# Attention scores over stacked high and low parts, and weighing in 32 bits

## The reference

```
x = x + 0.5 * ffn(layernorm(x))
x = x + attention(layernorm(x))
x = x + 0.5 * ffn(layernorm(x))
```

```
q, k, v = inputs @ w_q.T, inputs @ w_k.T, inputs @ w_v.T     # 16 heads of 16
scores = einsum('bqhd,bkhd->bhqk', q, k)                     # causal, -inf above the diagonal
attn = softmax(scores / sqrt(256))
ctx = einsum('bhqk,bkhd->bqhd', attn, v)
return ctx @ w_o.T + b_o
```

## Time and profile before

| | |
|---|---|
| median of 3 runs | 439.52 us (436.39 to 440.93) |
| the profiled execution | 440.74 us |
| its span, first to last instruction | 438.6 us |
| TensorE busy | 408.5 us (93%) |
| DVE, ACT, GpSimd busy | 300.8, 257.1, 247.7 us |
| mean granted TensorE clock | 0.973 of full speed |
| attention stage | from about 161 to 292 us |

### The profile page before, as it was taken

The page is one execution under the profiler, slowest core; times in us unless marked ns, Lnnn a source line. Parts: engine busy times, 40 slices in busy tenths (PEclk is TensorE's granted clock), DMA queues, the critical chain, the costliest instruction groups (busy, mean ns, idle before and its releaser), DMA issues.

```text
span 438.6 us, 10176 instructions
## 1 busy us (share of the span) xinstructions
PE 408.5 (93%) x2911; PEld 333.9 (76%) x2912; DVE 300.8 (69%) x613; ACT 257.1 (59%) x638; POOL 247.7 (56%) x307
## 2 busy tenths in 40 slices
PE   7768999999999889799999999888799999999996
PEld 4536888888888867588887888764488888888884
DVE  6767996865556697777677676966365575556566
ACT  2706885555655455788787787822155655655552
POOL 5136445866467349657777577210365586754850
PEclk9679999999999999989999999996999999999999
DMA  8929931111211630000000000007551212112136
GB/s 278 371 68 347 389 100 59 47 51 60 59 48 36 190 109 1 1 1 2 4 1 0 0 0 0 1 1 252 153 184 49 62 37 72 60 48 52 44 103 208
DMA packets 25738, 38.90 MB, mean 89 GB/s; under 512 B 3056, under 2 KB 20720, under 8 KB 25712
## 3 DMA queue, kind: packets, MB, share of 16 engines
q1 hardware_dynamic: 19088, 24.41, 16.3%
q0 software_dynamic: 4544, 12.07, 9.4%
q10 hardware_dynamic: 2080, 2.10, 1.4%
HBM read 29.37 MB, written 9.19 MB: 88 GB/s over the span
## 4 chain that ended last, share of the span: by engine, by line
PE 65%; DVE 12%; DMA 10%; issue 5%; ACT 3%; POOL 2%; SPq 1%; DVEq 0%; ACTq 0%; POOLq 0%
PE bank L1301 24%; PE bank L1323 12%; PE bank L1459 7%; PE bank L1470 4%; PE bank L1311 3%; DMA xn_scratch<-arena 3%; PE bank L1224 3%; DMA w_out<-y_scratch 3%; PE bank L1426 2%; PE bank L1277 2%; PE bank L1506 2%; DMA arena<-xn_scratch,gather_row 2%; DVE w_lo L876 1%; DMA y_scratch<-arena,scatter_row 1%; PE bank L1460 1%
## 5 line engine op out<-in xcount | busy, mean ns | idle before, releaser
L509 POOL DMA_INDIRECT arena<-xn_scratch,gather_row x46 | 50.8, 1105 | 72.7 <-PE bank L1277 42.1
L515 POOL DMA_INDIRECT y_scratch<-arena,scatter_row x42 | 60.2, 1434 | 34.3 <-ACT arena L681 31.2
L1301 PE MATMUL bank<-w_hi,xT_hi 128*128 x184 | 62.6, 421 | 1.2 <-ACT xT_hi L640 1.2
L990 DVE TENSOR_TENSOR wo_lo<-w_out,wo_hi 128x1024 fp32r<-128x1024 f32 x46 | 60.8, 1321 | 4.1 <-PE bank L1323 1.9
L995 DVE TENSOR_TENSOR gT_lo<-bank,gT_hi 128x512 fp32r<-128x512 f32 x46 | 31.7, 689 | 39.3 <-ACT gT_hi L655 39.2
L1301 PE MATMUL bank<-w_hi,xT_lo 128*128 x184 | 58.1, 397 | 0.0
L1301 PE MATMUL bank<-w_lo,xT_hi 128*128 x184 | 57.8, 395 | 0.0
L593 POOL TENSOR_TENSOR k_head<-k_hi,head_mask 128x256 fp32r<-128x256 f32 x64 | 38.7, 625 | 29.1 <-PE bank L1460 22.2
L648 ACT ACTIVATE arena<-bank 128x512 f32<-128x512 f32 x46 | 27.5, 598 | 45.7 <-PE bank L1301 45.7
L670 ACT ACTIVATE wo_hi<-w_out 128x1024 fp32r x46 | 48.8, 1060 | 6.0 <-issue 4.1
L979 DVE TENSOR_TENSOR xT_lo<-bank,xT_hi 128x256 fp32r<-128x256 f32 x46 | 19.5, 424 | 39.0 <-ACT xT_hi L640 38.9
(11 more groups left out here) (180 smaller groups left out, 968.8 us busy)
## 6 DMA issues: line engine op xcount, KB each, us to landing
w_raw<-in_win_t SPq DMA_DIRECT2D x8, 1024.0 KB, 9.7
w_out<-in_wout_t SPq DMA_DIRECT2D x16, 512.0 KB, 8.0
w_out<-y_scratch SPq DMA_DIRECT2D x16, 256.0 KB, 4.9
xn_scratch<-arena ACTq DMA_DIRECT2D x2, 1024.0 KB, 8.7
x<-in_x SPq DMA_DIRECT2D x4, 256.0 KB, 3.6
out<-x SPq DMA_DIRECT2D x4, 256.0 KB, 2.1
arena<-xn_scratch,gather_row POOLq DMA_INDIRECT x46, 3.5
y_scratch<-arena,scatter_row POOLq DMA_INDIRECT x46, 3.0
```

The source lines that it names most:

```text
L509: pool.indirect_dma_start(out=xb[j % 2][:, :], out_offset=None, in_=xn_dram, in_offset=bass.IndirectOffsetOnAxis(ap=gather_row[:, j:j + 1] ...
L515: pool.indirect_dma_start(out=y_dram, in_=y[j % 2][:, :], in_offset=None, out_offset=bass.IndirectOffsetOnAxis(ap=scatter_row[:, j:j + 1], ...
L990: dve.tensor_tensor(wo_lo[:, :, :], w_out[:, bass.ds(e, 1), :, :].rearrange("p o c d -> p (o c) d"), wo_hi[u][:, :, :].bitcast(F32), ALU.s ...
L1301: last = pe.matmul(bank[2 * half + u][:, :], tok[u][:, k, :], wts[:, bass.ds(e, 1), k, half * H:(half + 1) * H], start=(part == 0 and k == ...
```

## The change

- **Scores.** The heads of a chunk are laid out anew (`lay_heads` permutes the weights' columns) so that a group of 64 rows holds 4 heads as (number within the head, head). SP then copies, from SBUF to SBUF, each half of the chunk into `q_stack` and `k_stack`: 16 rows of `q_hi`, 16 of `q_hi` again, 16 of `q_lo`, against `k_hi`, `k_lo`, `k_hi`. A head's score is now one product over 48 rows (0 to 47 or 64 to 111) that sums all three parts. Each copy is 64 rows of 1 KB; there are 12 for each chunk. `mask_keys` and `k_head` are gone. Head scores also use 256 columns for each head (`HEAD_KEYS`), into banks 2 and 6 in turn.
- **Weighing.** `v` and the turned probabilities stay 32-bit; each head and block has one product of 16 columns. The turned probabilities are only copied, one head on DVE and one on ACT. Context sums lie in bank 5 alone, and `divide` is one DVE multiplication from that bank.
- **Order.** The loop over batches is written out as 32 + 3 steps. A chunk is projected five pairs ahead. Values of tiles 0 to 3 come ahead of the first scores, the rest in steps 0 and 1. Head maxima and exponentials stand in the next step. At the end the next normalisation's turns stand in the last steps, and most expert scores ahead of the last projection.

The diff, cut to its core:

```diff
+CHUNKS = BATCH * DK
+QPAIRS = BATCH * HPAIRS
+GROUP, STACK = P // 2, 3
+GROUP_HEADS = HPC // 2
+HEAD_KEYS = SEQ
-CONSTS = 21
+CONSTS = 18
+CHUNK_AHEAD = 5
+VBANK = (6, 4, 5, 3)
+HBANK = (2, 6)
+TURN_LAG, WEIGH_LAG = 2, 3
+DIVIDE_LAG = HPAIRS - 1 + WEIGH_LAG + 1
...
+            def stack(kk):
+                c = kk % DK
+                q_stack, k_stack = stacks[c]
+                sp.wait_ge(k_hi_ready, kk + 1)
+                sp.wait_ge(qk_ready, kk + 1)
+                for g in range(2):
+                    if kk >= DK:
+                        sp.wait_ge(head_scored, (kk - DK) * CPAIRS + CPAIRS - 1 + g)
+                    rows = slice(GROUP * g, GROUP * (g + 1))
+                    for n in range(STACK):
+                        at = slice(GROUP * g + HD * n, GROUP * g + HD * (n + 1))
+                        for to, part in ((q_stack, (q_hi, q_hi, q_lo)[n][c]), (k_stack, (k_hi, k_lo, k_hi)[n][:, c, :])):
+                            if to is q_stack:
+                                part = part[:, :, :].rearrange("p q t -> p (q t)")
+                            sp.dma_start(to[at, :, :].bitcast(F32), part[rows, :].bitcast(F32)).then_inc(stacked[c][g], 16)
...
+            def copy_turned(g):
+                act.wait_ge(probsT_done, 2 * g + 2)
+                reach(act, pv_done, 2 * (g - 2) + 2)
+                act.activation(pT[g % 2 * 2 + 1][:, :, :], bank[4][:, 0:3 * P].rearrange("p (k t) -> p k t", k=3), ACT.Copy)\
+                    .then_inc(pT_ready[1], 1)
...
+            def divide(b):
+                dve.wait_ge(pv_done, HEADS * (b + 1))
+                reach(dve, ctxT_done, b)
+                dve.reciprocal(inv_sum[:, :, :], row_sum[:, b, :, :]).then_inc(sums_inverted, 1)
+                dve.wait_ge(sums_inverted, b + 1)
+                dve.tensor_tensor(ctxv[:, :, :, :].rearrange("p q h d -> p (q h) d"),
+                                  bank[5][:, :].rearrange("p (h d) -> p h d", d=HD),
+                                  bc(inv_sum[:, :, :].rearrange("p q h -> p (q h)"), 2, [P, 2 * HEADS, HD]), ALU.mult)\
+                    .then_inc(ctx_ready, 1)
...
+                for g, to, tile, width, _ in jobs:
+                    q_stack, k_stack = stacks[g // CPAIRS % DK]
+                    rows = slice(g % 2 * GROUP, g % 2 * GROUP + STACK * HD)
+                    for hh in range(2):
+                        s = g % CPAIRS // 2 * 2 + hh
+                        pe.matmul(to[:, hh * SEQ:hh * SEQ + width], q_stack[rows, s, tile * P:(tile + 1) * P],
+                                  k_stack[rows, s, 0:width], start=(hh == 0), stop=False, skip_group_check=True)
+                for g, to, tile, _, scored in jobs:
+                    pe.matmul(to[:, :].rearrange("p (h k) -> p h k", h=2)[:, :, tile * P:(tile + 1) * P], ident_b[:, :],
+                              bc(neg_mask[:, :], 1, [P, 2, P]), start=False, stop=True, skip_group_check=True)\
+                        .then_inc(scored, 1)
...
+            def weigh(g):
+                b, p = g // HPAIRS, g % HPAIRS
+                if p == 0:
+                    reach(pe, ctx_ready, b)
+                for hh in range(2):
+                    h = head(p, hh)
+                    pe.wait_ge(pT_ready[hh], g + 1)
+                    for i, (qt, kt) in enumerate(((0, 0), (1, 0), (1, 1))):
+                        last = pe.matmul(bank[5][:, qt * D + h * HD:qt * D + (h + 1) * HD], pT[g % 2 * 2 + hh][:, i, :],
+                                         v[:, 2 * b + kt, h, :], start=(kt == 0), stop=(kt == qt), skip_group_check=True)
+                    last.then_inc(pv_done, 1)
...
+            def attend():
+                chunk(0)
+                values(0, 2)
+                turn(1, (1,))
+                chunk(1)
+                turn(1, (2,))
+                pe.wait_ge(x_added, TILES - 2)
+                values(2, 4)
+                pe.wait_ge(x_added, TILES)
+                for n in range(QPAIRS + WEIGH_LAG):
+                    if n < QPAIRS:
+                        scores(n, None)
+                    if n == 0:
+                        turn(1, (3,))
+                        values(4, 6)
+                    elif n == 1:
+                        values(6, 8)
+                    if 0 <= n - TURN_LAG < QPAIRS:
+                        turn_probs(n - TURN_LAG)
+                    if n < QPAIRS:
+                        scores(None, n)
+                    if n >= WEIGH_LAG:
+                        weigh(n - WEIGH_LAG)
+                    if (n + CHUNK_AHEAD) % CPAIRS == 0 and DK <= (n + CHUNK_AHEAD) // CPAIRS < CHUNKS:
+                        chunk((n + CHUNK_AHEAD) // CPAIRS)
+                    if n > DIVIDE_LAG and (n - DIVIDE_LAG - 1) % HPAIRS == 0:
+                        turn_context((n - DIVIDE_LAG - 1) // HPAIRS)
+                    if n > DIVIDE_LAG + 1 and (n - DIVIDE_LAG - 2) % HPAIRS == 0:
+                        project_out((n - DIVIDE_LAG - 2) // HPAIRS)
+                    if n >= QPAIRS + 1:
+                        turn(2, (n - QPAIRS - 1,))
+                pe.wait_ge(attn_added, BATCH - 1)
+                warm(WARM_CONTEXT, 7)
+                turn(2, (TPAIRS - 2,))
+                turn_context(BATCH - 1)
+                score_experts(1, range(TPAIRS - 2))
+                project_out(BATCH - 1)
+                score_experts(1, (TPAIRS - 2,))
+                warm(WARM_SCORES)
```

More of the change, by code:

```diff
@@ L352, in reach, with head @@
                 eng.wait_ge(signal, count)
[L354 to L368, removed]
+        def head(p, hh):
+            return p // CPAIRS * HPC + p % 2 * GROUP_HEADS + p % CPAIRS // 2 * 2 + hh
         def bc(ap, axis, shape):
@@ L579, in _ @@
                     add_bias(1, bo, i - 1, 1)
[L581 to L606, removed]
+            add_bias(1, bo, TPAIRS - 2, 2)
             inverse_root(2, 0, TPAIRS - 1)
@@ L830, in _, with copy_context @@
-            sweep(act, step)
+                                   accum_out=row_sum[:, b, 0, head(p, hh):head(p, hh) + 1]).then_inc(head_probs_ready, 1)
+            def copy_turned(g):
[3 more added lines that the diff above has]
+                    .then_inc(pT_ready[1], 1)
+            def copy_context(b):
+                act.wait_ge(ctxT_done, b + 1)
+                act.activation(ctxT[:, :, :], bank[7][:, :].rearrange("p (k t) -> p k t", k=DK), ACT.Copy)\
+                    .then_inc(ctxT_ready, 1)
@@ L831, in _ @@
+            attend()
             ffn(1)
@@ L1490, in turn_context, with scores @@
[L1490 to L1495 removed]
+            def scores(tail, head):
+                jobs = []
+                if tail is not None:
+                    kk, g = tail // CPAIRS, tail % 2
+                    pe.wait_ge(stacked[kk % DK][g], 16 * 2 * STACK * (kk // DK + 1))
+                    if tail < 2:
+                        pe.wait_ge(xnT_ready, TPAIRS + tail + 3)
+                    reach(pe, tail_probs_ready, 2 * (tail - 2) + 2)
+                    jobs.append((tail, bank[tail % 2], 1, SEQ, tail_scored))
+                if head is not None:
+                    if head == 1:
+                        pe.wait_ge(v_ready, 5)
+                    reach(pe, head_probs_ready, 2 * (head - 2) + 2)
+                    jobs.append((head, bank[HBANK[head % 2]], 0, HEAD_KEYS, head_scored))
+                for g, to, tile, width, _ in jobs:
[9 more added lines that the diff above has]
+                        .then_inc(scored, 1)
@@ new lines, in turn_probs @@
+            def turn_probs(g):
+                if g == 0:
+                    pe.wait_ge(v_ready, TILES)
+                for hh in range(2):
+                    pe.wait_ge(head_probs_ready, 2 * g + hh + 1)
+                    reach(pe, pT_ready[hh], g)
+                    for i in range(3):
+                        last = pe.transpose(bank[3 + hh][:, i * P:(i + 1) * P], probs[g % 2][:, hh, i, :], ident[:, :])
+                    last.then_inc(probsT_done, 1)
+            def weigh(g):
+                b, p = g // HPAIRS, g % HPAIRS
+                if p == 0:
+                    reach(pe, ctx_ready, b)
+                for hh in range(2):
+                    h = head(p, hh)
[4 more added lines that the diff above has]
+                    last.then_inc(pv_done, 1)
```

409 lines of the change are left out of this document (134 added, 275 removed).

## The result

The changed kernel takes 493.37 us (median of 4 runs, 483.55 to 497.49) against 439.72 us (4 runs, 436.39 to 440.93): the ratio is 1.109, 95% interval 1.092 to 1.127. The forecast was 436, its range ended at 450. The profiled execution of the changed kernel is the fastest of its four: 483.55 us, span 481.7, mean granted clock 0.904, where before had 438.6 and 0.973. The other three spans are 488.9, 494.2 and 495.7 at clocks of 0.883, 0.875 and 0.872: the time goes with the clock.

The account below looks back on a forecast made before the run. TensorE's unbroken stream was taken as the bound: -2.7 - 0.2 - 0.5 - 1.5 = -4.9, plus 1.6 for row changes, gave -3.3 on the profiled 440.74, so 437.4, and 436 for the median; range 428 to 450.

Parts of the forecast that it names:

- The bound: Attention stage: only TensorE has no room, busy 19.84 of 20 us; work saved on other engines shortens nothing.
- rival (2): Attention pairs: TensorE's clock falls to 1.2 GHz in half of them, +16 us, 452 in all; chance 0.11.
- changes of rows: TensorE switching between 48-row and 128-row products, four times a pair: 0.05 us a pair, +1.6 us in all.
- Rival (1): Score pairs: each first product after a change of rows is 0.10 us late, 12.8 us instead of 1.6, 447; chance 0.16.
- its own gain of 4.9 us: Whole kernel: sum of the expected savings, -2.7 - 0.2 - 0.5 - 1.5, before the cost of row changes.
- the 1% of the chances: Whole kernel: differences under about 1%, 4.4 us, count as the same; slower means above 443.9 us.
- The place of the head scores: Attention pair: head scores behind the transposes are TensorE's order already, so their place costs nothing by itself.
- The pair's own work: One pair of heads on TensorE: scores and masks 0.84, transposes 0.58, weighing 1.30, together 2.72 us, 0.22 more than before.
- The breaks: Pair 8 to pair 31: of 8.0 us of gaps in TensorE's stream 2.0 remain, so 6.0 come back.
- Pair 31 to the best experts: End of attention through expert choice: 0.5 us saved before the last projection, about 1.5 behind it; 21.3 us forecast.
- The copies: SP's twelve copies a chunk: issued 0.54 us apart, in time when steady; TensorE waits about 1.5 us at the start.
- Pair 8: Start of the attention stage: its tail scores begin at 196.8 us instead of 197.01, a gain of 0.2.

Follow-up runs that it names:

- warm2: Changed kernel plus two useless 512-column products of ones over 128 rows for each pair of heads; 464.37 us.
- warm2_48: Changed kernel plus two useless 512-column products of ones over 48 rows for each pair of heads; two runs of 534.66 and 547.35 us.
- rows128: Changed kernel with a fourth copy and score products over all 128 rows instead of 48, so its scores are not the reference's; 455.30 us, ratio 1.038.
- warm1: Changed kernel plus one useless 512-column product of ones over 128 rows for each pair, ahead of the transposes; 456.26 us, ratio 1.040.
- rows64: Changed kernel with a fourth copy (low by low) and score products over 64 rows instead of 48; two runs of 467.43 and 488.37 us.

## Why the prediction was wrong, step by step

**The bound.** Right: TensorE alone. It is busy 20.00 of 20 us, waits for no DVE or ACT instruction between 180 and 320, and what left DVE, ACT and GpSimd shortened nothing.

**The step that failed: the clock had no term in the sum.** The prediction took 2.4 GHz for granted wherever TensorE is busy, though its own rival (2) had rows that speak against this: full busy time, short columns, clock 0.50 soon after. It set them aside because scores, masks and transposes stand between. They do, but the scores are over 48 rows with a change of rows on either side, and warm2 against warm2_48 shows that products placed like that do not keep the clock up. The Trainium skill, "TensorE: Matmul & The Clock Gate", Part 1, says that the clock follows how busy the array has lately been; this trace agrees only if busy is not read as the profile's busy column, which stood at 20.00 in each 20-us stretch from 180 to 300. Rival (2) was also priced too low. It doubled only the 1.0 us of streaming; the whole pair grows 1.8 times, from 3.19 to 5.76, weight loads included. At a clock of 0.78 about 44% of the time is spent at 1.2 GHz (0.78 = 1 - 0.5 x 0.44). The loss of 33 to 38 us stands where the rival had 16.

**The term that was mis-sized: changes of rows.** Allowed 0.05 a pair, measured 0.46 (3.18 against 2.72 by rows128), so 14.7 us instead of 1.6. Rival (1)'s mechanism and its 0.10 a change were about right: 0.08 to 0.16 each, 14.7 us for its 12.8. It was wrong only in placing the cost in the first product after a change alone: 0.24 lies there, ahead of the first score product, and 0.22 between that product and the mask behind it. Its remark that the kernel is slower from 0.07 a change on holds only if slower means by the 1% of the chances; its own gain of 4.9 us is used up at 4.9 / 128 = 0.04. Rivals (1) and (2) came true together, a case that had no price. The Trainium skill, "TensorEngine Tiling (Array Packing)", Key Properties, says that a change of tiling mode drains TensorE; these runs agree as far as they show a delay at the changes, some 0.12 us each. The place of the head scores was called free because it was TensorE's order already. It was free before, when nothing changed rows there.

**The pair's own work.** Right: 2.72 forecast, 2.72 measured where no rows change. Weighing 1.26 to 1.34 for 1.30; score products 0.16 each in rows128 for 0.155.

**The breaks.** Right as far as the clock lets it be seen. With the product of ones, 23 pairs at 3.40 (3.18 + 0.22) instead of 2.50 and one chunk fewer would make 80.3 + 20.7 - 1.75 = 99.3; measured 92.6, so 6.7 us came back where 6.0 had been forecast. The division hides beside the next pair as said (reciprocal at 221.05, product at 221.44, both done before the weighing at 222.79). Pair 31 to the best experts took 21.6 for 21.3.

**The copies.** Right in the steady stretch: they land in 2.6 us, and TensorE never waits for one from 180 on. At the start it waits 1.73 and 1.20 us, and the term that was a little small is the pace of the issues: 0.64 us apart (SP's start at 166.75, 167.46, 168.09 and so on) for 0.54. Pair 8 starts at 200.4 in warm1, 202.6 if its earlier start of 2.2 us is added, for 196.8; row changes and ones explain some 4 of these 6 us (six pairs by 0.46 + 0.22).

With the measured row changes, 437.4 + 13.1 = 450.5 would have been forecast for a profiled execution at 2.4 GHz; warm1 without its ones gives 455.28 - 7.0 = 448.2, and 450.4 with the 2.2 us of its earlier start. So these two steps, 13 and 33 us, account for the whole miss of 46 (483.55 - 437.4). **Open:** whether the clock answers to the rows at work or to the changes of rows, why it falls just where it does, whether rows64 helps it, and what late copies cost in rows128.

## What to carry to other kernels

Where a change replaces long products over all rows on TensorE by products over part of the rows, write down a term for the clock even if TensorE stays busy, and test it by adding a useless long product over all rows: if the kernel gets faster, the clock was the cost. Count changes between 128 and fewer rows as instructions of about 0.12 us (the mean here), and put products of one shape next to each other. Work saved on other engines is worth nothing until TensorE's own sum of a step goes down.

## What the runs showed of the hardware that was not expected

- A stream without a gap ran at 1.2 GHz: 20.00 of 20 us busy at a mean clock of 0.59, and 0.51 in warm2_48.
- One more 512-column product over 128 rows a pair, 0.22 us of work, and the clock read 1.00 from 160 to 300 us; two over 48 rows made the kernel 70 us slower than two over 128.
- The same products in another order, with two row changes a pair instead of four, raised the clock over 180 to 300 us from 0.78 to 0.90.
- At 1.2 GHz a 32-bit product of 16 columns takes 0.20 us for each of its two instructions instead of 0.11, though it streams only 16 columns; its loads take 2.66 us for twelve instead of 1.43.
- Products over 64 rows pay the same at the changes as products over 48.
